# A fourth B and C buffer, matmuls in place of two trips through DRAM, constants on three queues and a new table of places in a Mamba, retention and expert layer

## The reference

```python
# Mamba: D_INNER = 256, D_STATE = 16, DT_RANK = 8
x_b, z = split(x @ W_in)
xc = silu(conv_b + causal 4-tap convolution of x_b)
delta_raw, B_in, C_in = split(xc @ W_xproj)
delta = softplus(delta_raw @ W_dt + b_dt)
A_bar = exp(delta[..., None] * A)
Bx = delta[..., None] * B_in[:, :, None, :] * xc[..., None]
h = a_t * h + bx_t;  y_t = einsum('bds,bs->bd', h, c_t) + D_param * xc_t     # per step t
x1 = layernorm(x + (y * silu(z)) @ W_out)
# retention: queries from x1, keys and values from the context
x2 = layernorm(x1 + ((rot(x1 @ Wq) @ rot(ctx @ Wk).T) * decay_mask) @ (ctx @ Wv))
# experts: 16 of width 64, the best two with softmax weights, and a shared one of width 128
out = layernorm(x2 + sum_k combine[k] * down_k(silu(gate_k(x2)) * up_k(x2)) + shared(x2))
```

## Time and profile before

| | us |
|---|---|
| median of 3 runs | 1173.52 |
| lowest, highest | 1171.49, 1175.31 |
| the profiled execution, whole | 1174.27 |
| its span, first to last instruction | 1172.2 |
| busy: PE, DVE, ACT, POOL | 1055.3, 1065.3, 993.9, 972.0 |
| mean granted TensorE clock, share of full speed | 0.967 |

### The profile page before, as it was taken

One profiled execution on the slowest core, in us unless ns is written; L12 is line 12 of the kernel. 1 busy time (PEld: TensorE's weight loads), 2 busy tenths in 40 slices (PEclk: granted clock), 3 DMA queues, 4 the chain that ended last, 5 costly groups with the idle time before them and its releaser, 6 DMA issues. The chain is left out here.

```text
span 1172.2 us, 18321 instructions
## 1 busy us (share of the span) xinstructions
PE 1055.3 (90%) x5831; PEld 742.9 (63%) x5831; DVE 1065.3 (91%) x1492; ACT 993.9 (85%) x2176; POOL 972.0 (83%) x590
## 2 busy tenths in 40 slices
PE   4677888989899998989989899998989999898998
PEld 2465665666666666666666666666666667666665
DVE  2999999999999999999999999999999999999622
ACT  6788898989989898998979898898989889898443
POOL 0687888979988897988979798898989889897944
PEclk9677999999999999999989999999999999999999
DMA  6443444545564444555534455654545655443322
GB/s 173 175 171 146 163 164 158 164 164 189 198 196 156 172 162 153 188 207 190 182 127 168 163 189 187 204 175 162 159 160 178 208 187 182 144 166 144 122 68 74
DMA packets 84112, 194.50 MB, mean 166 GB/s; under 512 B 17288, under 2 KB 47936, under 8 KB 67632
## 3 DMA queue, kind: packets, MB, share of 16 engines
q1 hardware_dynamic: 84016, 193.33, 48.8%
HBM read 179.14 MB, written 5.77 MB: 158 GB/s over the span
## 5 line engine op out<-in xcount | busy, mean ns | idle before, releaser
L936 POOL TENSOR_TENSOR read<-state,bc_all 128x1024 f32<-128x1024 f32 x256 | 604.0, 2364 | 140.8 <-DVE state L805 126.3
L805 DVE TENSOR_TENSOR_SCAN state<-decay,drive_bank 128x512 f32<-128x512 f32 (+1 forms) x464 | 594.7, 1313 | 0.4
L755 ACT ACTIVATE decay<-delta,a_neg 128x252 f32<-128x252 f32 x1024 | 424.6, 494 | 0.9
L797 DVE TENSOR_TENSOR drive_bank<-dx_bank,bc_all 128x512 f32<-128x512 f32 (+1 forms) x496 | 328.9, 701 | 27.6 <-DMA bc_all<-bc_dram 25.8
L372 PE MATMUL y_bank<-ident,read 128*128 128x128 f32 x2048 | 282.6, 283 | 44.9 <-POOL read L936 44.8
L372 PEld LDWEIGHTS y_bank<-ident,read 128*128 128x128 f32 x2048 | 241.7, 146 | 118.9 <-POOL read L936 80.8
L977 POOL TENSOR_TENSOR hid<-gu,comb_all 128x512 f32<-128x512 f32 (+1 forms) x136 | 165.0, 1214 | 22.5 <-DVE gu L897 18.8
L363 PEld LDWEIGHTS down_bank<-down_w,hid 128*128 128x128 f32 x1024 | 132.3, 196 | 37.0 <-issue 28.1
L363 PE MATMUL bank<-x2T,gate_w 128*128 128x512 f32 (+1 forms) x272 | 135.0, 588 | 9.8 <-ACT delta L735 4.3
L363 PE MATMUL down_bank<-down_w,hid 128*128 128x128 f32 x1024 | 139.1, 281 | 3.0 <-POOL hid L977 1.4
L363 PE MATMUL bank<-x2T,up_w 128*128 128x512 f32 (+1 forms) x272 | 130.0, 571 | 0.8 <-ACT xc L711 0.7
(11 more groups left out here) (128 smaller groups left out, 1385.0 us busy)
## 6 DMA issues: line engine op xcount, KB each, us to landing
bc_all<-bc_dram SPq DMA_DIRECT2D x128, 1024.0 KB, 5.3
comb_all<-comb_dram SPq DMA_DIRECT2D x240, 128.0 KB, 3.0
x_in<-in_x_dram SPq DMA_DIRECT2D x15, 256.0 KB, 5.7
ctx_in<-in_ctx_dram SPq DMA_DIRECT2D x15, 256.0 KB, 6.4
k_pair<-k_pair SPq DMA_DIRECT2D x30, 128.0 KB, 2.1
q_pair<-q_pair SPq DMA_DIRECT2D x30, 128.0 KB, 2.5
out_dram<-y_out SPq DMA_DIRECT2D x15, 256.0 KB, 3.1
comb_all<-comb_dram SPq DMA_DIRECT2D x32, 64.0 KB, 2.6
```

Source lines behind the costliest of these rows:

```text
L755: done = e.activation(seqs(decay_t[j % DECAYS][:, i, h, :])[:, :, 1:T], seqs(delta[c % 2][:, h, sub * SUB:(sub + 1) * SUB])[:, :, 1:T], AC ...
L797: e.tensor_tensor(drive_bank[:, a:b, :, :], dx_bank[:, :, :].unsqueeze(1).to_broadcast(shape), bc_all[group % BC_BUFS][:, 0, PAIR * i + a: ...
L805: e.tensor_tensor_scan(states(state_t[j % STATE_BUFS], a, b), states(decay_t[j % DECAYS], a, b), states(drive_bank, a, b), 0.0, ALU.mult, ...
L936: e.tensor_tensor(read_t[j % READS][:, :, :, :], state_t[j % STATE_BUFS][:, :, :, :], bc_all[group % BC_BUFS][:, 1, PAIR * i:PAIR * (i + 1 ...
```

## The change

Six edits, and a new table.

- bc_all gets a fourth buffer. The memory comes from writing in place: y_gated becomes gate_z, k_t and q_t become the first halves of k_pair and q_pair. The load of a group is still issued 16 ticks ahead (`BC_AHEAD = 2`).
- The B and C of the first group (steps 0 and 1) no longer go through DRAM. PE spreads them by eight matmuls with a column of the identity as broadcast weights into down_bank and y_bank, DVE copies them into bc_all[0]. DVE, not ACT, copies the first proj, and computes the first dx straight into dx_bank.
- The expert weights of chunk 16 no longer go through DRAM. PE spreads them by eight matmuls of 256 columns (weight_mm) into drive_bank, dx_bank and y_bank, with a selector that DVE builds in a decay buffer, and DVE, not POOL, multiplies them into hid.
- Constants go out on three queues: SP, ACT (ident, a_log, conv_w, conv_b) and POOL (w_out, down_w). Those that are used late are issued by SP in the course of the ticks. What each instruction waits for is counted apart.
- w_out and down_w are centered right after the first convolution on DVE, ahead of the copy of the first proj.
- ACT loads its tables for exp, silu and softplus early in the head, by an activation of one column each.
- AT and EXP_AT have five columns: chunks in the middle (as before), 16, 15, 0 and 1.

```diff
-DECAYS, STATE_BUFS, READS, BC_BUFS, COMBS = 7, 2, 2, 3, 3
+DECAYS, STATE_BUFS, READS, BC_BUFS, COMBS = 7, 2, 2, 4, 3
+BC_AHEAD = 2
+COLUMN = [3, 4] + [0] * (CHUNKS - 4) + [2, 1]
-    "bc_store": [(-31, -27)],
+    "bc_store": [(-31, -22, -28, -21, -33)],
-        y_gated = sb("y_gated", [P, SUBS, SUB_BLOCKS, INNER])
-        q_t, k_t = sb("q_t", [P, CHUNK]), sb("k_t", [P, CHUNK])
 # PE, at dt_mm
+                    if c == 0:
+                        for two in (0, 1):
+                            for pair in (0, 1):
+                                w.wait_ge(S["bc_copy"], 2 * two + pair - 1)
+                                for i in range(PAIR):
+                                    row = DT_RANK + GROUP * pair + PAIR * two + i
+                                    done = mm((down_bank, y_flat)[pair][:, i * SUB:(i + 1) * SUB],
+                                              ident[0:PROJ, row:row + 1].to_broadcast([PROJ, P]), proj[0:PROJ, 0:SUB])
+                                done.then_inc(S["bc_mm"], 1)
 # PE, tail
+                for c, pair in due(tick, "weight_mm"):
+                    if c < LAST:
+                        continue
+                    w.wait_ge(S["combT"], at(c))
+                    w.wait_ge(S["state"], PAIR * STEPS)
+                    w.wait_ge(S["y_gated"], ALL_SUBS)
+                    w.wait_ge(S["selector"], 1)
+                    mm(last_weight(pair), selector[0:EXPERTS, pair * P:(pair + 1) * P],
+                       combT[:, 0:SUB]).then_inc(S["weight_mm"], 1)
 # ACT, ahead of the ticks
-            w.wait_ge(S["first_consts"], 16 * 6)
+            e.dma_start(ident[:, :], io["c_ident"]).then_inc(S["ident"], 16)
+            e.dma_start(a_log[:, :, :], ...).then_inc(S["a_log"], 16)
+            e.dma_start(conv_w[:, :, :], ...).then_inc(S["conv_consts"], 16)
+            per_channel(e, conv_b, io["L0_attn_conv_b"], S["conv_consts"])
+            warm(0, ACT.Exp)
 # DVE
-                        (0, -3, ((w_out[:, :, :], 0, HALVES), (down_w[:, :, :], HALVES, PAIRS))),
+                        (0, CENTER_TICK, ((w_out[:, :, :], 0, HALVES), (down_w[:, :, :], HALVES, PAIRS))),
+                    e.tensor_tensor(hid[index % 3][:, 0:SUB], gu[index % 2][:, 0:SUB], last_weight(pair),
+                                    ALU.mult).then_inc(S["last_hid"], 1)
 # POOL, ahead of the ticks
+            e.dma_start(w_out[:, :, :], ...).then_inc(S["out_consts"], 16)
+            e.dma_start(down_w[:, :, :], ...).then_inc(S["out_consts"], 16)
 # SP
+                if tick == 1:
+                    e.dma_start(ctx_t[1][:, 0:blocks_of(1), :], rows_of(io["ctx_1024"], 1)).then_inc(S["ctx_load1"], 16)
+                    e.dma_start(gate_w[:, :, :], ...).then_inc(late, 16)
+                    e.dma_start(up_w[:, :, :], ...).then_inc(late, 16)
-                if tick % (GROUP_STEPS * TICKS) == 0 and 0 <= (group := tick // (GROUP_STEPS * TICKS) + 2) < ALL_SUBS * GROUPS:
+                if tick % (GROUP_STEPS * TICKS) == 0 and 0 < (group := tick // (GROUP_STEPS * TICKS) + BC_AHEAD) < ALL_SUBS * GROUPS:
...
```

More of the change, by code:

```diff
@@ new lines @@
+    "bc_store": [(-31, -22, -28, -21, -33)],
+    "k_swap": [(65, 43, 63, 30, 64)],
+    "q_swap": [(75, 60, 77, 41, 75)],
+    "comb_store": [(130, 137, 127, 98, 130)],
+    "x_load": [(-56, -88, -59, -54, -61)],
+    "ctx_load": [(-47, -53, -62, -48, -65)],
+    "store": [(229, 237, 209, 193, 228)],
+    "z_mm": [(12, 16, 12, -23, 6), (37, -39, 37, 17, 37)],
+    "gate_z": [(10, 22, 10, -21, 4), (40, 31, 39, 16, 40)],
+    "y_gated": [(38, 58, 37, 11, 37), (69, -20, 69, 36, 69)],
+    "yT_mm": [(60, 62, 54, 28, 61), (69, 8, 69, 37, 69)],
@@ L288, in blocks_of, with loads @@
             return width(c) // P
+        def loads(buffer, groups):
+            return uses(groups, buffer, BC_BUFS) - (1 if buffer == 0 else 0)
         def uses(before, buffer, buffers):
@@ L777, in _ @@
                             tap_rows.rearrange("p (n k) -> p k n", k=TAPS), ALU.mult).then_inc(S["w_tap"], 1)
+            w.wait_ge(S["ident"], 16)
             e.tensor_scalar(center[:, :], ident[:, :], 1.0, -1.0 / D, ALU.mult, ALU.add)
             for tick in range(FIRST_TICK, LAST_TICK):
-                if tick == -36:
-                    w.wait_ge(S["early_consts"], 16 * 11)
+                for c in due(tick, "proj"):
+                    if c > 0:
+                        continue
+                    w.wait_ge(S["proj_mm"], 1)
+                    e.tensor_scalar(proj[:, 0:SUB], bank_of["proj", 0][0:PROJ, 0:SUB], 1.0, 1.0, ALU.mult, ALU.mult).then_inc(
+                        S["proj"], 1)
+                for c, sub in due(tick, "dx"):
+                    if c > 0:
+                        continue
+                    bc_copy(0, 0)
+                    w.wait_ge(S["delta"], 2)
+                    w.wait_ge(S["xc"], HALVES)
+                    e.tensor_tensor(dx_bank[:, :, :], xc[0][:, :, 0:SUB], delta[0][:, :, 0:SUB],
+                                    ALU.mult).then_inc(S["first_dx"], 1)
+                    bc_copy(0, 1)
+                    bc_copy(1, 0)
+                    bc_copy(1, 1)
+                    w.wait_ge(S["d_consts"], 16 * 2)
@@ L898, in _ @@
                                     ALU.mult).then_inc(S["gu"], 1)
+                for c, pair in due(tick, "hid"):
+                    if c < LAST:
+                        continue
+                    index = pair + 1
+                    w.wait_ge(S["gu"], at(c, index, TILES))
+                    w.wait_ge(S["weight_mm"], pair + 1)
+                    w.wait_ge(S["down_mm"], at(c, index - 3, TILES))
+                    e.tensor_tensor(hid[index % 3][:, 0:SUB], gu[index % 2][:, 0:SUB], last_weight(pair),
+                                    ALU.mult).then_inc(S["last_hid"], 1)
         @block.gpsimd
```

327 lines of the change are left out of this document (206 added, 121 removed), and 5 rows, old and new, of the table EXP_AT.

## The result

| | before | changed |
|---|---|---|
| median, us (17 runs each) | 1174.13 | 1182.73 |
| lowest to highest | 1167.20 to 1179.91 | 1175.29 to 1194.08 |
| profiled execution | 1174.27 | 1176.87 |

The changed kernel is slower: ratio 1.0071, 95% interval 1.0050 to 1.0093, some 8 us. Its times spread more, and the execution that was profiled is one of its shortest.

The account below looks back on a forecast made before the run. The prediction took DVE as the bound, with less than 2 us to win per middle chunk. It summed 1174.3 + 0 (middle) - 3.8 (head) - 0.4 (tail) = 1170.1, less 0.8 is 1169.3 us; range 1152 to 1180.

Parts of the forecast that it names:

- no gain in the middle: Middle chunks: awaited loads stay behind comb_all in SP's order, so 0 us, between a gain of 23.3 and a loss of 26.
- the head's -3.8: Head: net gain of 3.8 us after a later load takes back part of the earlier first scan; between -8.0 and +2.3.
- the tail's -0.4: Tail: -2.0 for gate_z, -1.8 of idle time, +3.4 for eight matmuls; between -4.5 and +3.4.
- Rival A: Middle: the fourth buffer does remove DVE's waits for B and C; -23.3 us more, 1146; 15 in 100.
- Rival B: Middle: an earlier load slows the awaited one on shared DMA engines; 13 chunks lose 13 us, 1182; 14 in 100.
- 22.9 in my sum: Head: first scan at 22.9 us instead of 30.88, 8.0 gained.
- The first term: Head, up to xT: earlier PE start and ACT table load give 3.5 us, xT ready at 5.3.
- The load of steps 4 and 5: Head: now behind the store of chunk 1's proj, it goes at 35.4, drive at 40.7; 4.5 of the 8.0 left.
- Rival C: Head gained whole, the load of step 4 being early enough; -8.0 and -0.4 give 1165.1; 9 in 100.
- D: Head and tail give back what they win: head -0.7, tail +1.4, 1174.2; 8 in 100.
- the 2.0: Tail: PE's wait of 2.00 us for gate_z removed, -2.0, or 0 if PE then waits for something else.
- its 3.4 us: Tail: eight added 256-column matmuls at 0.43 us each cost +3.4 in full if PE has no idle time there.

Follow-up runs that it names:

- x3_early_mid: Changed kernel with the loads of B and C issued 5 ticks earlier from tick 19 on; ratio 0.9883 to the kernel before.
- x1_wait3: Changed kernel with each load of B and C waiting for the same read as with three buffers; ratio 1.0108 to the kernel before.
- z1_all: Changed kernel with B and C loads 5 ticks earlier everywhere, last expert weights and first B and C through DRAM; ratio 0.9818 to the kernel before, median 1151.37 us.
- the second trace: The changed kernel profiled once more, nothing altered; this execution took 1183.80 us.
- v2_before_shift: Kernel before, three buffers, with its loads of B and C issued 2 ticks earlier; ratio 1.0003 to the kernel before.
- e2_tail_store: Changed kernel with the last expert weights through DRAM and the load of steps 4 and 5 ahead of chunk 1's proj store; ratio 1.0029 to the kernel before.
- y1_tail_dram: Changed kernel with the last chunk's expert weights through DRAM again instead of the eight weight_mm; ratio 1.0016 to the kernel before.
- v3_shift_tail: Changed kernel with B and C loads 5 ticks earlier everywhere and last expert weights through DRAM, first B and C by matmuls; ratio 0.9814 to the kernel before.
- x4_early_all: Changed kernel with the loads of B and C issued 5 ticks earlier everywhere, head included; ratio 0.9876 to the kernel before.

## Why the prediction was wrong

The forecast of no gain in the middle held. What failed are the head's -3.8, whose first scan came too late and whose sum stopped before the chunks that follow, and the tail's -0.4, which had no term for TensorE's clock.

**The middle: right.** No gain from the fourth buffer as the change uses it, since SP's order holds the awaited loads. Forecast 20 us or more of waits with the issue right behind comb_all; found 28.9 us, of which 23.3 outside the head as before, and 641.10 behind 639.97. Rival A fell as changed, but its price was well judged: x3_early_mid gained some 22 us, of the 23.3 that I named, once the loads moved. Rival B fell with x1_wait3.

**The head: wrong in sign.** Forecast -3.8 us, kept to the end; at step 32 the two traces stand at +3.6 and +5.4, and all ten with the middle as changed at +2.2 to +8.8. Three things failed.

- The first scan, 22.9 in my sum, came at 25.1 in the first trace and at 29.7 in the second. The first term was right: xT was ready at 5.34 (4.98 + 0.36), forecast 5.3. But I had the weights there by then, and PE's first matmul on xT waited 2.87 us for the taps' weights, to 7.02. proj_mm ended at 13.76 in place of 11.4 and delta at 15.91 in place of 14.8, 1.1 us late. The other half of the 2.2 us is the spreading matmuls. I had priced them at DVE's copies alone, between 12.7 and 20.6, "in DVE's wait for the convolution". They stand on PE ahead of chunk 1's first matmul: groups of 1.02 to 1.13 us at full speed and 1.91 to 2.07 at half, and in the first trace the clock fell during the fourth (1.56). Chunk 1's first matmul then takes 2.07 us, against 1.13 in z1_all without them, and ACT waits 1.06 us for it. In the second trace that wait is 3.58 us. That PE may be at half speed in the head can be seen in the earlier trace rows: proj_mm takes 1.06 us for 256 columns and 3.63 for 512. I took each duration in its own state.
- The load of steps 4 and 5 went at 37.50 instead of 35.4, the drive at 43.15 instead of 40.7. The mechanism was right (the store ahead of it); most of the 2.4 us is the late convolution of the first point (22.86 instead of 20.6) handed on.
- What I had not summed at all: the steps of chunk 1 and the first half of chunk 2. From step 8 (-0.7) to step 32 (+3.6) the changed kernel loses 4.3 us more. PE idles, and then its clock falls: granted 0.79 from 140 to 156 us, where the kernel before has 1.00. The rows of the changed kernel, PE and then DVE:

```profile
146.65 6.32 PE L399 MATMUL bank<-xT,w_tap 128*128 128x512 f32 x8 [2.60 <-ACT silu L807]
...
153.49 0.42 DVE L1011 TENSOR_TENSOR gu<-silu,bank 128x256 f32<-128x256 f32 x1 [2.57 <-issue]
```

The eight matmuls take 6.32 us. In the two traces with the old table (the kernel before and v2_before_shift) the taps at this place have no idle time ahead of them and take 3.52. In all 16 with the new table PE idles 2.6 us there, and in 14 of them the taps take 5.07 to 6.51 us, in the other two (the second trace and e2_tail_store) 3.62. From step 16 to 32 the fourteen lose 0.1 to 5.1 us against the kernel before, and the two gain 0.4 and 0.5. So the idle time comes with the new table, and the fall of the clock mostly with it. It does not tell slow kernels from fast ones: z1_all has it too, with 5.32. The new table gives the chunks at the start other places; I looked only at what the table moved in the first 45 us. What this stretch costs to the end rests on reading: no run puts the old places back alone.

Rival C falls with the drive at 43.15, which had to come before 38. D had its drive at 44.5, and 43.15 lies between that and my 40.7; its time, 1174.2, lacks the early chunks and the clock as my own does.

**The tail: too good.** Forecast -0.4 us for the whole. PE's wait for gate_z did go (the x2T gate matmul at 1094.14 has none), though PE then waits 1.48 us for POOL's read and 0.51 for hid, so not all of the 2.0 was kept. weight_mm cost its 3.4 us. Where the clock held, the terms came out: the rest of the span was 70.9, against 70.7 before. In six of seven traces with 16 rows it was 73.6 to 74.6. The term that was missing is the clock, 2.7 to 3.7 us. Without weight_mm the rests are 69.0 to 69.8, and the ratio falls by 0.0055 (y1_tail_dram) and by 0.0062 (v3_shift_tail against x4_early_all), 6 to 7 us; that the clock is the larger part of it rests on the traces.

The Trainium skill ("TensorE: Matmul & The Clock Gate", "Part 1: The HAM clock gate (the "warmup" mystery)") says that the clock follows how busy TensorE has been. In the second trace it was busy, by the profile, 20.00 of 20.00 us and its clock fell; there the measurement decides. What differed from the three traces with 128 rows, which all held it, was the number of rows of eight matmuls.

**The sum.** Tail undone, 1.0016; the stall at step 4 undone as well, 1.0029. So the tail is over half of the 0.7%, shown by runs. What is left, 0.2 to 0.3% by these two, I put to the early chunks and the head's matmuls by reading, not by a run. Nor did a run take back the writing in place, which every variant of the changed kernel keeps; the kernels at 0.98 have it too. The 8.0 us that the first scan was to gain, and the 5.8 that it did in the first trace, don't come from the matmuls, since the trip through DRAM starts as early; no run separates the other edits of the head. From step 48 to the last scan the traces of kernels with the changed middle drift from -5 to +9 us against the kernel before, so a single trace can't settle a share of a few us there.

## What to carry over

A buffer more gives time only if the queue that issues its loads gets to them earlier: look at what stands ahead of the load in the issuing engine's order, and move the load with the buffer (0.9876 with both, 1.0071 with the buffer alone; in the fastest kernel 0.9818 with both and 1.0046 with the place alone). A trip through DRAM replaced by matmuls puts TensorE, in whatever clock state it is there, on the path; price such matmuls at both speeds, and ask what the clock does behind them. When a change brings a new table of places, read the first chunks on all engines to the point where both kernels run alike.

## What was unexpected

- TensorE's granted clock fell to 0.83 over 20 us without any idle time, behind eight matmuls of 16 rows (six traces of seven), and never behind the same eight over 128 rows (three of three).
- The granted clock can read 1.00 where the durations show half speed: 1.93 instead of 1.06 us for the same four matmul records in the head. Ahead of the trace's first clock record the view has nothing to go by.
- The same program's head comes out in two states, with the first scan near 25 or near 30 us, as TensorE's clock first rises at 11 to 13 or at 30 us, while the time of the whole shows no such step.
- Landings of 7.1 us in place of 5.3 cost nothing that could be measured.
